# A fourth buffer for the streamed second feed-forward weight, in a state-space plus quantized feed-forward layer on eight cores

## The reference, cut to what matters

```python
# per sequence: x is [4096, 1024]
x = x + layernorm(attn(layernorm(x), W_in, W_sel_in, W_sel_out, W_out, d_param))
x = x + layernorm(ffn(layernorm(x), w1, conv_w, conv_b, w2))

def attn(x, ...):      # a gated linear recurrence over the tokens, state 256
    u = x @ W_in.T; g = silu(x @ W_sel_in.T) @ W_sel_out.T
    a, b, c, dg = sigmoid(g0), tanh(g1), tanh(g2), sigmoid(g3)
    h_t = a_t * h_{t-1} + (b * u)_t
    return (c * h + d_param * dg * u) @ W_out.T

def bit_linear(x, w):  # x quantized to 8 bits per token, w to -1, 0, 1 (times one scale)
    return act_quant(x) @ weight_quant(w).T

def ffn(x, w1, conv_w, conv_b, w2):     # hidden size 4096
    h = bit_linear(x, w1)                       # [4096, 4096]
    h = silu(depthwise_conv_3_taps(h) + conv_b) # along the tokens
    return bit_linear(h, w2)                    # [4096, 1024]
```

## Time and profile before

| | us |
|---|---|
| runs of the kernel before | 3280.07 median, 3271.27 to 3299.03, three runs |
| the profiled execution | 3277.29 |
| its span, slowest core (core 7) | 3275.7 |
| the other cores | 3256.0 to 3273.4 |
| PE busy | 1539.8 (47%) |
| DVE busy | 1476.8 (45%) |
| ACT busy | 1335.2 (41%) |
| POOL busy | 531.4 (16%) |
| DMA queue q1 (SP's), share of 16 DMA engines | 21.1% |

### The profile page before, as it was taken

One profiled execution on the slowest core, in us unless ns is written; L12 is line 12 of the kernel. 1 busy time (PEld: TensorE's weight loads), 2 busy tenths in 40 slices (PEclk: granted clock), 3 DMA queues, 4 the chain that ended last, 5 costly groups with the idle time before them and its releaser, 6 DMA issues.

```text
span 3275.7 us, 35704 instructions; the slowest of 8 cores (3256.0 to 3275.7 us)
## 1 busy us (share of the span) xinstructions
PE 1539.8 (47%) x8464; PEld 884.2 (27%) x8464; DVE 1476.8 (45%) x5002; ACT 1335.2 (41%) x2201; POOL 531.4 (16%) x817
## 2 busy tenths in 40 slices
PE   0000026464646464646464546464646565555454
PEld 0000014041414141414142424242423233332230
DVE  1024426262636354545445453636362626273452
ACT  1544434343435343434444343434343434343332
POOL 0000010202020202020202021211111121212202
PEclk9999967577777777878777878787877777778885
DMA  6777600304030303031312122221212121212213
GB/s 199 224 214 219 170 23 1 106 17 106 23 106 23 106 23 105 24 94 35 87 42 75 54 69 61 61 68 53 77 52 78 52 78 39 78 39 77 65 52 100
DMA packets 112701, 260.35 MB, mean 79 GB/s; under 512 B 12656, under 2 KB 12656, under 8 KB 112496
## 3 DMA queue, kind: packets, MB, share of 16 engines
q1 hardware_dynamic: 93200, 196.19, 21.1%
q10 hardware_dynamic: 13824, 41.95, 4.4%
q0 software_dynamic: 5472, 19.93, 2.2%
HBM read 232.85 MB, written 25.17 MB: 79 GB/s over the span
## 4 chain that ended last, share of the span: by engine, by line
PE 23%; DVE 22%; DMA 16%; ACT 14%; issue 10%; DVEq 8%; POOL 4%; ACTq 2%; POOLq 1%; SPq 0%
DMA w2sb<-w2s 10%; PE pE L872 8%; DVEq L58 8%; DVE h L915 4%; PE pD L1061 4%; DVE h L923 3%; POOL h L1045 3%; PE pE L1061 3%; DMA tad<-w2T 3%; ACT h L887 2%; DVE h L907 2%; PE pC L550 2%; DMA tbc<-w2T 2%; ACT hpre L881 2%; PE pB L542 1%
## 5 line engine op out<-in xcount | busy, mean ns | idle before, releaser
L872 PE MATMUL pE<-xqw,w1t 128*128 128x258 bf16 x4352 | 599.7, 301 | 316.2 <-ACT h L887 312.3
L1061 PE MATMUL pD<-w2sb,h 128*128 128x512 bf16 x1024 | 350.8, 429 | 487.6 <-POOL h L1045 296.7
L872 PEld LDWEIGHTS pE<-xqw,w1t 128*128 128x128 bf16 x4352 | 459.4, 107 | 440.3 <-issue 342.1
L881 ACT ACTIVATE hpre<-pE 128x258 bf16<-128x258 f32 x544 | 198.8, 387 | 457.0 <-DVE h L923 354.9
L1045 POOL TENSOR_SCALAR h<-k2i,consts 128x512 bf16<-128x512 int32 x272 | 265.8, 985 | 613.7 <-ACT k2i L1041 613.7
L1061 PE MATMUL pE<-w2sb,h 128*128 128x512 bf16 x1024 | 347.0, 426 | 37.6 <-POOL h L1045 22.3
L1041 ACT ACTIVATE k2i<-h,consts 128x512 int32<-128x512 bf16 x272 | 192.7, 720 | 352.2 <-DVE h L1030 255.6
L826 DVE COPY xqw<-xqw 128x8 bf16<-128x8 bf16 x16 | 3.0, 185 | 620.5 <-ACT xqw L819 620.5
L1061 PEld LDWEIGHTS pD<-w2sb,h 128*128 128x128 bf16 x1024 | 80.0, 103 | 734.9 <-issue 727.5
L915 DVE SCALAR_TENSOR_TENSOR h<-hpre,cwt,h 128x256 bf16<-128x256 bf16 x544 | 227.4, 480 | 10.3
L923 DVE SCALAR_TENSOR_TENSOR h<-hpre,cwt,h 128x256 bf16<-128x256 bf16 x544 | 227.3, 479 | 10.5 <-issue 0.4
(11 more groups left out here) (183 smaller groups left out, 2108.7 us busy)
## 6 DMA issues: line engine op xcount, KB each, us to landing
w2sb<-w2s SPq DMA_DIRECT2D x544, 256.0 KB, 3.0
tad<-w2T ACTq DMA_DIRECT2D x32, 512.0 KB, 5.4
xin<-x SPq DMA_DIRECT2D x16, 1024.0 KB, 7.0
tbc<-w2T ACTq DMA_DIRECT2D x32, 512.0 KB, 4.7
stgF<-w1T POOLq DMA_DIRECT2D x32, 512.0 KB, 4.8
stgF<-w1T SPq DMA_DIRECT2D x32, 512.0 KB, 5.4
out<-stgF SPq DMA_DIRECT2D x32, 512.0 KB, 3.2
w2s<-stgb ACTq DMA_DIRECT2D x16, 256.0 KB, 5.0
```

The source lines that it names most:

```text
L872: lambda e, S, c=c, k=k, off=off, pf=pf: e.matmul(pE[:, off:off + 258], w1t[:, 4096 * k + 128 * c:4096 * k + 128 * (c + 1)], xqv[:, pf, k, :],
L881: q.op("a", lambda e, S, c=c, off=off: e.activation(hpre[:, 258 * (c % 4):258 * (c % 4 + 1)], pE[:, off:off + 258], AF.Identity), sem="ac")
L1061: coff=coff: e.matmul(bank[:, 512 * jj:512 * (jj + 1)], h4[:, 256 * c + 128 * s:256 * c + 128 * (s + 1)], w2sb[:, coff:coff + 512], start= ...
```

## The change

`w2sb` gets a fourth buffer: 4096 instead of 3072 columns, 2 KB more in each partition. Chunk c goes to buffer c % 4, with a fourth semaphore `sw3`. A window starts with four loads instead of three, and `issue_w2t(c + 4)` stands where `issue_w2t(c + 3)` was. The loads, their size and number, the matmuls and all other lists are the same.

```diff
-        w2sb = sb("w2sb", [128, 3072], BF16)
+        w2sb = sb("w2sb", [128, 4096], BF16)
@@
             def issue_w2t(c):
                 if c >= 32:
                     return
-                if f == 0 and c < 3:
+                if f == 0 and c < 4:
                     q.wait("sy", "swi", sw_w2)
-                if c >= 3:
-                    q.wait("sy", "pe", PE_w2c[f][c - 3])
+                if c >= 4:
+                    q.wait("sy", "pe", PE_w2c[f][c - 4])
                 elif f > 0:
-                    q.wait("sy", "pe", PE_w2c[f - 1][29 + c])
-                swn = "sw%d" % (c % 3)
+                    q.wait("sy", "pe", PE_w2c[f - 1][28 + c])
+                swn = "sw%d" % (c % 4)
                 SW_w2t[f][c] = (swn, q.op("sy", lambda e, S, c=c: e.dma_start(
-                    out=w2sb[:, 1024 * (c % 3):1024 * (c % 3 + 1)],
+                    out=w2sb[:, 1024 * (c % 4):1024 * (c % 4 + 1)],
                     in_=w2s[:, 1024 * c:1024 * (c + 1)]), sem=swn, k=16))

             issue_w2t(0)
             issue_w2t(1)
             issue_w2t(2)
+            issue_w2t(3)
@@
-                        coff = 1024 * (c % 3) + 512 * jj
+                        coff = 1024 * (c % 4) + 512 * jj
@@
                 PE_w2c[f][c] = mm
-                issue_w2t(c + 3)
+                issue_w2t(c + 4)
```

More of the change, by code:

```diff
@@ L38, in __init__ @@
                                    "swi", "gd", "gp", "pe", "dv", "ac",
-                                   "ad", "vd", "sw2")}
+                                   "ad", "vd", "sw2", "sw3")}
     def do(self, qn, f):
@@ L136, in build_program @@
         for s in ("sm", "sx0", "sx1", "so", "sw0", "sw1", "swi", "gd", "gp",
-                  "pe", "dv", "ac", "ad", "vd", "sw2"):
+                  "pe", "dv", "ac", "ad", "vd", "sw2", "sw3"):
             sems[s] = st_.enter_context(nc.semaphore(s))
```

## The result

| | kernel before | changed kernel |
|---|---|---|
| median of 10 runs each, us | 3274.85 | 3189.34 |
| ratio to before, 95% interval | | 0.9742, 0.9722 to 0.9761 |
| span of the slowest core in the profiled execution, us | 3275.7 (core 7) | 3186.7 (core 4) |
| mean of the eight cores' spans, us | 3262.9 | 3176.8 |

The change makes the kernel 2.6% faster. The forecast was 3187 us, with 3150 to 3235 us as the range. The total is 2.3 us above the forecast. The gain is 85.5 us where the sum had 92 us: with seven more runs the median of the kernel before moved from 3280.07 to 3274.85 us, and this hides the rest in the total.

What follows compares the result with a forecast made beforehand. The prediction took part B's wait for w2 loads, latency divided by three buffers, as the bound. Savings of 75 + 8.4 + 8.1 = 92 us from 3277.3 us gave 3185 us, stated as 3187 us for the median, range 3150 to 3235 us.

Steps and rivals of the forecast that it cites:

- The loop: Part B of W2: load latency over buffer count sets the pace, 1.45 us per chunk with three, 1.14 with four.
- Latency with four in flight: Part B's loads: 0.2 us more latency than now, a loop of 4.55 us instead of 4.35 us.
- The first three chunks: Start of part B: granted clock 0.5 holds these chunks at 1.7 us each, 5.07 us together; no gain.
- The fifteen parts B in sum: Part B of windows 0 to 14: 5.0 us saved in each, 75 us together.
- Windows 15 and 16: W2 of the last two windows: faster chunks save 8.4 us in window 15 and 8.1 us in window 16.
- Part A at nothing: Part A, windows 0 to 14: some 3 us faster, hidden behind DVE's attention piece, so costed at nothing.
- The bound by the DMA engines: Part B's loads: DMA engines busy 0.88 us per chunk, bounding the pace at about that value.
- B: Rival for the loads: latency grows with load, pace 1.23 to 1.40 us, gain 13 to 60 us, about 3240 us; chance 0.16.
- my case: The forecast's main case for W2's loads: pace 1.05 to 1.23 us, gain 60 to 120 us; chance 0.66.
- A: Rival for the loads: the queue adds nothing, pace 0.93 to 1.05 us, gain 120 to 155 us, about 3140 us; chance 0.10.
- C: Rival for part B: something else right behind bounds it, so no change, about 3277 us; chance 0.05.
- D: Rival for part B: PE's granted clock falls back to 0.5, 70 us lost, about 3350 us; chance 0.03.

## Why the prediction was right, point by point

**What bounds the kernel: right.** The chain of waits led to part B, and all of the gain is in the places that it named: 69.7 us in fifteen parts B, 16.1 us in windows 15 and 16.

**The loop: right.** With two, three and four buffers every chunk waits for its load, and the pace falls with the number of buffers (2.21, 1.43, 1.21 us). The forecast gave the pace within 6%: 1.14 forecast, 1.21 measured.

**Latency with four in flight: undersized.** This is the term that was mis-sized. I added 0.2 us to the loop, 4.55 us. Measured is 4.83 us, 0.54 us over the 4.29 us of before (0.39 us from issue to use, 0.07 us of release, the rest from averaging). The pace gained 0.22 instead of 0.31 us per chunk, 3.3 instead of 4.7 us over 15 chunks: 20 us too much in the forecast. The sign for it, 3.1 to 3.3 us to landing, came out at 3.6 us. The prediction's last paragraph calls its mechanism wrong if the latency grows with the number of loads. Taken by its words this sign came true, although the sum itself had put 0.2 us of growth in. The runs say that the mechanism, the loop, holds and that the growth was priced at half.

**The first three chunks: wrong, and it paid back most of that.** I put their 5.07 us down to the clock and costed them at no gain. In the mean over windows they took 4.77 us, and the run with load 15 in place took 4.26 us: the load cost 0.5 us, and the slow clock 4.26 - 3 x 0.86 = 1.7 us. The rows had it: load 15 can only be issued behind chunk 12, 2 us into part B (1620.73 us), and needs 3 us. With four buffers it is chunk 16, not 15, that meets this limit, so the sign "first three chunks still 5.1 us" failed too (4.2 us in window 6, 4.15 us on average). Chunk 12 to 16 took 1.36 us less, of which the forecast had 0.31 us: 1.05 x 15 = 16 us too little.

**The fifteen parts B in sum** were forecast at 75 us and gave 69.7 us: 20 us too much and 16 us too little nearly cancel. The total was good partly by luck. Without the 16 us it would have been some 3205 us, still inside the range.

**Windows 15 and 16: right.** 8.4 and 8.1 us forecast, 7.7 and 8.4 us measured. **Part A at nothing: right**, 3 us faster and hidden, PE's pause at 19.57 us as said. The DMA share from 1593.5 to 1613.5 us was 0.75, inside the 0.72 to 0.82. **The load of x**: it started at 1570.33 us, behind part A's loads, and part B's first issue was at 1591.58 us; they did not meet.

**The bound by the DMA engines: wrong as a floor.** 0.88 us per load from the share was no floor; eight buffers went to 0.69 us over ten microseconds of window 16. The 0.88 us was also a slip: it divides by 17 chunks, but 178 GB/s over 23.43 us are 15.9 loads, 0.94 us each (0.93 from the packets). Neither did harm, because the loop was the limit. By the Trainium skill's figure ("DMA: Bandwidth & Descriptors", "Anatomy of one DMA") a load takes an estimated 2.6 us; the loads from SBUF took 2.3 us, those from device memory 3.0 to 3.6 us, so with memory as the source the page's figure is too short here.

**The rivals.** B, latency that grows with load, is what happened in kind but not in size: the pace stayed below its 1.23 us. Its 3.6 us to landing were reached, and its loop of 4.9 us nearly, so my case and B met at their border. The page of the Trainium skill that the prediction cited there ("DMA: Bandwidth & Descriptors", "Latency and other measured facts") has device memory's latency rise under load; the runs show the direction (3.0 to 4.2 us to landing from three to six buffers), not its cause. A, C and D did not happen. PE's clock in part B of window 6 was 0.93 where it had been 0.91.

**Two readings that were off and changed nothing.** The load of x ran at 344 to 410 GB/s for 2 us, not 3. The first use of the loads at a window's start is some 75 us later, not 65: window 7's are issued from 1675.57 us on, and its W2 begins at 1753.16 us.

## What to carry to other kernels

Where a stream of loads waits for its buffers, follow one buffer once round: from the use to the next issue to the next use. That time over the number of buffers is the pace, and it tells something only if the loads are used as soon as they land; a chunk that lies ready means that the consumer or something else is the limit. The time round grew with the fourth buffer here (4.3 and 4.8 us for three and four), so it brought less than its share. When SBUF is nearly full, look for tiles that are idle during the stage: two of them took this kernel from 0.974 to 0.942.

## What the runs showed of the hardware that I had not expected

- A load of 256 KB from device memory took longer with more buffers (2.7, 3.0, 3.6, 4.2 us to landing in the median of the slowest core with two, three, four, six), while the same load from SBUF stayed at 2.3 us with three and four. With more buffers there are more loads in flight and also more bytes per microsecond; no run tells these two apart. With eight, where PE set the pace, it grew no further (3.8 us in the median for `w2sb`).
- A DMA share of 0.64 is no measure of what is left: the engines went from 0.93 us of packet time per load to a load in 0.69 us over ten microseconds in which their share was 1.01 (eight buffers, window 16).
- With waits of 0.8 to 1.5 us between chunks of four matmuls, PE's granted clock dropped to 0.5 and back inside one stage (two buffers); in window 6 of the kernel before, with a pace of about 1.4 us per chunk, it stayed at 1.00 from 1623.84 us to the end of part B.
